# Another order of pieces, maxima and banks in the heads stage of a fused attention and experts kernel

## What is computed

```
xn = layernorm(x)
# branch 1: time mixing, then channel mixing
xc  = ln(ln(x2)); xcs = shift(xc)
kc  = square(relu(xcs @ Wck))            # 512 -> 2048, "up"
vc  = kc @ Wcv                           # 2048 -> 512, "down"
out1 = x2 + sigmoid(xc @ Wcr) * vc
# branch 2: causal attention in 4 x 16 heads of 32, then experts
p   = softmax(causal(q @ k.T * scale)); h = p @ v
x3  = xn + h @ Wo.T                      # "proj"
out2 = x3 + experts(rmsnorm(x3))
out = x + out1 + out2
```

## Time and profile before

| | |
|---|---|
| median of 3 executions | 1740.48 us (1737.22 to 1743.84) |
| the profiled execution, its own time | 1737.22 us |
| its span, first to last instruction | 1735.5 us |
| busy over the span: PE, DVE, ACT, POOL | 93%, 59%, 53%, 28% |
| mean granted TensorE clock | 0.983 |

### The profile page before, as it was taken

One profiled execution on the slowest core, in us unless ns is written; L12 is line 12 of the kernel. 1 busy time (PEld: TensorE's weight loads), 2 busy tenths in 40 slices (PEclk: granted clock), 3 DMA queues, 4 the chain that ended last, 5 costly groups with the idle time before them and its releaser, 6 DMA issues.

```text
span 1735.5 us, 26111 instructions
## 1 busy us (share of the span) xinstructions
PE 1621.6 (93%) x9014; PEld 1348.2 (78%) x9014; DVE 1021.1 (59%) x1980; ACT 917.4 (53%) x1649; POOL 480.0 (28%) x647
## 2 busy tenths in 40 slices
PE   3978899999989999999999899999999999999996
PEld 2756677877767777766768789898989898989895
DVE  7787742236665555655454655757565757575652
ACT  6465653334644655545643235656565656565652
POOL 4353320100111211211211312334342424252432
PEclk9999999999999999999999999999999999999998
DMA  6354576889796765974576665858585867676761
GB/s 239 101 172 150 214 216 188 240 253 311 229 291 190 212 193 121 297 222 124 155 233 213 213 190 193 281 201 269 199 275 200 271 221 252 235 239 229 246 230 25
DMA packets 119219, 370.12 MB, mean 213 GB/s; under 512 B 30175, under 2 KB 30175, under 8 KB 105378
## 3 DMA queue, kind: packets, MB, share of 16 engines
q1 hardware_dynamic: 98850, 329.36, 56.8%
q0 software_dynamic: 15696, 31.21, 9.7%
q10 hardware_dynamic: 4592, 8.52, 1.3%
HBM read 289.47 MB, written 85.72 MB: 216 GB/s over the span
## 4 chain that ended last, share of the span: by engine, by line
PE 64%; DVE 5%; ACT 3%; DMA 3%; issue 2%; SPq 1%; POOL 0%; DVEq 0%; POOLq 0%; ACTq 0%
PE bank L53 18%; PE bank L54 18%; PE bank L55 18%; PE bank L2283 3%; PE bank L2260 2%; PE bank L2248 2%; DVE ex_w_lo L2689 1%; DMA st_qk<-hd_max_rows 1%; DVE hd_a L2060 1%; PE bank L2792 1%; ACT hd_a_hi L1933 1%; DVE hd_masked L2120 1%; DMA st_qk<-scratch_qk 1%; PE bank L2352 1%; ACT hd_relu L1912 1%
## 5 line engine op out<-in xcount | busy, mean ns | idle before, releaser
L2689 DVE TENSOR_TENSOR ex_w_lo<-ex_stage,ex_w_hi 128x1024 fp32r<-128x1024 f32 x207 | 248.7, 1235 | 171.4 <-ACT ex_w_hi L2599 166.7
L2525 POOL TENSOR_TENSOR ex_a_lo<-ex_a,ex_a_hi 128x256 fp32r<-128x256 f32 x128 | 92.5, 746 | 292.9 <-ACT ex_a_hi L2621 292.7
L53 PE MATMUL bank<-ex_x_hi_a,ex_w_hi 128*128 128x256 f32 x512 | 145.0, 283 | 0.3 <-DVE ex_a L2727 0.3
L53 PE MATMUL bank<-ex_x_hi_b,ex_w_hi 128*128 128x256 f32 x512 | 144.6, 282 | 0.0
L55 PE MATMUL bank<-ex_x_hi_b,ex_w_lo 128*128 128x256 f32 x512 | 144.1, 282 | 0.0
L54 PE MATMUL bank<-ex_x_lo_a,ex_w_hi 128*128 128x256 f32 x512 | 144.1, 281 | 0.0
L55 PE MATMUL bank<-ex_x_hi_a,ex_w_lo 128*128 128x256 f32 x512 | 144.1, 281 | 0.0
L54 PE MATMUL bank<-ex_x_lo_b,ex_w_hi 128*128 128x256 f32 x512 | 144.1, 281 | 0.0
L2596 ACT ACTIVATE ex_w_hi<-ex_stage 128x1024 fp32r<-128x1024 f32 x134 | 133.8, 1049 | 0.6 <-DMA ex_stage<-in_w_moe 0.6
L2120 DVE CUSTOM_DVE_ANT_0 hd_masked<-bank,causal 128x512 bf16<-128x512 f32 (+3 forms) x256 | 113.8, 484 | 26.2 <-PE bank L2248 26.2
L53 PE MATMUL bank<-ex_w_hi,ex_a_hi 128*128 128x512 f32 x312 | 126.1, 404 | 0.3 <-DVE ex_w_lo L2689 0.3
(11 more groups left out here) (313 smaller groups left out, 4515.0 us busy)
## 6 DMA issues: line engine op xcount, KB each, us to landing
ex_stage<-in_w_moe SPq DMA_DIRECT2D x69, 1536.0 KB, 7.1
first_w<-in_w_moe SPq DMA_DIRECT2D x23, 1536.0 KB, 7.0
hd_up<-scratch_up_halves SPq DMA_DIRECT2D x48, 512.0 KB, 6.8
hd_down<-scratch_down_halves SPq DMA_DIRECT2D x48, 512.0 KB, 6.1
st_qk<-scratch_qk SPq DMA_DIRECT2D x64, 256.0 KB, 4.9
st_qk<-scratch_qk SPq DMA_DIRECT2D x128, 64.0 KB, 4.9
scratch_up_halves<-hd_up SPq DMA_DIRECT2D x16, 512.0 KB, 3.9
scratch_down_halves<-hd_down SPq DMA_DIRECT2D x16, 512.0 KB, 3.8
```

Source lines behind the costliest of these rows:

```text
L53: pe.matmul(out, lhsT=w_hi, rhs=x_hi, start=first, stop=False)
L2525: pool.tensor_tensor(a_lo[:, chunk.par, m, :], a[:, m, :], a_hi[:, chunk.par, m, :].bitcast(F32), ALU.subtract).then_inc(wide_lo_ready, 1)
L2689: return dve.tensor_tensor(dst, src, hi.bitcast(F32), ALU.subtract)
```

## The change

The order of work within a step and the banks of the pieces are changed; the work itself is the same.
- `pieces_before`: between step 5 and step 64 there are 85 pieces instead of 88, spread as 85 * n // 59 instead of 3 * n // 2, so steps with one and with two pieces no longer alternate strictly with odd and even s; after step 64 there are two in each step. The proj pieces of two sequences come a few pieces earlier in `order`.
- Banks: ups use bank 5 and sums bank 6 (two for each kind among the first pieces and from TAIL on). A piece waits for the last piece of its own kind instead of for piece k - 2.
- Order in a step, on all three engines: the first piece (also when it is the only one) is begun and finished ahead of scores, maxima and exps of part 2; the second piece stands behind them. `pair_output` comes after scores 2. `turn_maxima` and `max_row` come at the end of step 4t + 3 instead of in step 4t + 4.

```diff
     def pieces_before(s):
         early = 2 * min(s, LAG)
-        middle = 3 * min(max(s - LAG, 0), N - LAG) // 2
-        late = (3 * max(s - N, 0) + 1) // 2
+        middle = 85 * min(max(s - LAG, 0), N - LAG) // (N - LAG)
+        late = 2 * max(s - N, 0)
...
-        def piece_bank(k):
-            return psum[5 + k % 2]
+        TWO_UPS, TWO_SUMS = pieces_before(LAG + 1), pieces_before(LAG)
+
+        def up_bank(k):
+            return psum[4] if (k >= TAIL or k < TWO_UPS) and ups_before[k] % 2 else psum[5]
+
+        def sum_bank(k):
+            if k < TWO_SUMS:
+                return psum[2] if sums_before[k] % 2 else psum[6]
+            return psum[0] if k >= TAIL and sums_before[k] % 2 != sums_before[PIECES - 1] % 2 else psum[6]
... (scalar)
-                if s % SET == 0 and 0 < s <= N:
-                    max_row(s // SET - 1)
-                for k in ks[:-1]:
+                for k in ks[:1]:
                     begin(k)
+                    finish(k)
+                if 0 <= i < N:
+                    exps(i, 2)
                 if 1 <= i <= N and i % 2 == 0:
                     inverse_sums(i // 2 - 1)
-                if 0 <= i < N:
-                    exps(i, 2)
-                for k in ks[:-1]:
-                    finish(k)
                 (take_v, high_o)
-                for k in ks[-1:]:
+                for k in ks[1:]:
                     begin(k)
                     finish(k)
+                if s % SET == SET - 1 and s < N:
+                    max_row(s // SET)
... (vector)
-                for k in ks[:-1]:
+                for k in ks[:1]:
                     begin(k)
+                    finish(k)
                 if s < N:
                     maxima(s, 2)
-                for k in ks[:-1]:
-                    finish(k)
-                for k in ks[-1:]:
+                for k in ks[1:]:
                     begin(k)
                     finish(k)
... (tensor: an up piece; total() does the same with sum_taken)
-                if k >= 2:
-                    pe.wait_ge(*taken(k - 2))
+                n = ups_before[k] - (k > TAIL + TT or 0 < ups_before[k] and k < TWO_UPS)
+                if k >= TAIL and n == ups_before[TAIL]:
+                    pe.wait_ge(o_ready, N)
+                if n:
+                    pe.wait_ge(a_full, n)
... (tensor)
-                if s % SET == 0 and 0 < s <= N:
-                    turn_maxima(s // SET - 1, misc_free[0])
-                    misc_free[0] = max_rows_ready, s // SET
-                if 2 <= i <= N and i % 2 == 0:
-                    pair_output(i // 2 - 1)
-                for k in ks[:-1]:
+                for k in ks[:1]:
                     piece(k)
                 if s < N:
                     scores(s, 2)
+                if 2 <= i <= N and i % 2 == 0:
+                    pair_output(i // 2 - 1)
                 if 0 <= i < N:
                     turned(i, 2)
-                for k in ks[-1:]:
+                for k in ks[1:]:
                     piece(k)
+                if s % SET == SET - 1 and s < N:
+                    turn_maxima(s // SET, misc_free[0])
+                    misc_free[0] = max_rows_ready, s // SET + 1
```

More of the change, by code:

```diff
@@ L1911, in begin @@
                     act.wait_ge(up_done, n + 1)
-                    act.activation(relu[:, m, :], piece_bank(k)[:, :], ACT.Relu).then_inc(relu_ready, 1)
+                    act.activation(relu[:, m, :], up_bank(k)[:, :], ACT.Relu).then_inc(relu_ready, 1)
                 for w in fresh[k]:
@@ L2059, in begin @@
                     dve.wait_ge(relu_ready, n + 1)
-                    dve.scalar_tensor_tensor(a[:, m, :], piece_bank(k)[:, :], 0.0, relu[:, m, :],
+                    dve.scalar_tensor_tensor(a[:, m, :], up_bank(k)[:, :], 0.0, relu[:, m, :],
                                              ALU.max, ALU.mult).then_inc(a_full, 1)
@@ L2067, in begin @@
                         dve.wait_ge(added, 16 * adds_before[order.index(("down", b - 1, CHUNKS - 1, DEEP - 1)) + 1])
-                    dve.tensor_copy(acc[:, m, :], piece_bank(k)[:, :]).then_inc(sum_taken, 1)
+                    dve.tensor_copy(acc[:, m, :], sum_bank(k)[:, :]).then_inc(sum_taken, 1)
                 elif kind == "down":
@@ L2071, in begin @@
                     dve.wait_ge(sum_taken, before + 1)
-                    dve.tensor_tensor(acc[:, m, :], piece_bank(k)[:, :], acc[:, m, :], ALU.add).then_inc(sum_taken, 1)
+                    dve.tensor_tensor(acc[:, m, :], sum_bank(k)[:, :], acc[:, m, :], ALU.add).then_inc(sum_taken, 1)
                     if c == CHUNKS - 1:
@@ L2080, in begin @@
                         dve.wait_ge(xn_in, b * 16 + 16)
-                    dve.tensor_tensor(xp[:, m, :], piece_bank(k)[:, :], xp[:, m, :], ALU.add).then_inc(sum_taken, 1)
+                    dve.tensor_tensor(xp[:, m, :], sum_bank(k)[:, :], xp[:, m, :], ALU.add).then_inc(sum_taken, 1)
                 for w in fresh[k]:
@@ L2255, in turned @@
                     pe.wait_ge(max_in, 16 * (i // SET + 1))
+                if n == 0:
+                    pe.wait_ge(sum_taken, sums_before[TWO_SUMS])
                 if n >= 2:
@@ L2275, in pair_output @@
                     pe.wait_ge(consts_ready, CONSTS)
+                    pe.wait_ge(a_full, ups_before[TWO_UPS])
                 else:
@@ L2294, in up_piece @@
                     pe.wait_ge(x_in, b * 32 + 32)
-                if k >= 2:
-                    pe.wait_ge(*taken(k - 2))
+                n = ups_before[k] - (k > TAIL + TT or 0 < ups_before[k] and k < TWO_UPS)
[3 more added lines that the diff above has]
+                    pe.wait_ge(a_full, n)
                 for q in range(HC):
-                    last = mm3(pe, piece_bank(k)[:, :], up_hi[:, m, q, :], up_lo[:, m, q, :], x_hi[:, q, 1:S + 1],
+                    last = mm3(pe, up_bank(k)[:, :], up_hi[:, m, q, :], up_lo[:, m, q, :], x_hi[:, q, 1:S + 1],
                                x_lo[:, q, 1:S + 1], q == 0, q == HC - 1)
@@ L2302, in total @@
             def total(k, left_hi, left_lo, j, ready):
-                if k >= 2:
-                    pe.wait_ge(*taken(k - 2))
+                n = sums_before[k] - (k > TAIL or 0 < sums_before[k] and k < TWO_SUMS)
+                if k == TAIL:
+                    pe.wait_ge(max_step, 3 * N)
+                if n:
+                    pe.wait_ge(sum_taken, n)
                 cols = slice(j * P, (j + 1) * P)
@@ L2308, in total @@
                         ready(q)
-                    last = mm3(pe, piece_bank(k)[:, :], left_hi(q)[:, cols], left_lo(q)[:, cols], down_hi[:, q, :],
+                    last = mm3(pe, sum_bank(k)[:, :], left_hi(q)[:, cols], left_lo(q)[:, cols], down_hi[:, q, :],
                                down_lo[:, q, :], q == 0, q == DEEP - 1)
```

2 lines of the change are left out of this document (removed).

## The result

The changed kernel takes 1803.84 us, median of 4 executions (1801.71 to 1810.70), against 1739.19 for the kernel before beside it (4 executions, 1737.22 to 1743.84): a ratio of 1.0375, 95% interval 1.0338 to 1.0411. It is slower by 65 us. The forecast was 1783 with a range of 1754 to 1808.

What follows compares the result with a forecast made beforehand. TensorE was taken to bound the heads stage, the only one touched. New costs 44.2 + 11.8 + 6 + 8 + 8 = 78 us, less 32 removed, gave +46 on 1737.2: 1783 us, range 1754 to 1808.

Steps and rivals of the forecast that it cites:

- Part 1: Steps 5 to 63: TensorE's score part 1 waits for part 2 maxima, now behind the first piece on VectorE: 44.2 us.
- Part 2: One bank for ups, one for sums: a piece waits for the last of its own kind, 11.8 us together.
- Part 3: Late steps with two pieces each: pieces wait 0.5 to 1.0 at eight places, 6 us (bounds 0 and 8).
- Part 4: Row maxima turned earlier, their DMA issued most of a step sooner: removes 3.8 us of waits.
- Part 5: Moved neighbours ahead of part 2: `choose` in steps 28 and 62, 6 us; xT copies and logits waits, 2.
- Removed: Old TensorE waits in the heads stage undone by Parts 1, 4 and 5: 32 us (bounds 15 and 32).
- Clock: Five more drops of TensorE to half clock in the heads stage: 8 us (bounds 0 and 20).
- A: Heads stage slower as summed, only sizes of covers and chains open: 1765 to 1798 us, chance 0.66.
- B: Clock follows each long wait: some 12 drops more, 20 us on top, 1798 to 1820; sign ten; chance 0.12.
- C: Waits overlap, one late VectorE answer paying for several TensorE waits: +15, 1746 to 1765 us, chance 0.12.
- D: Faster: part 2 maximum not late on VectorE, Parts 1 and 5 cost nothing: -14, 1723 us, chance 0.05.
- E: No net change: old waits were TensorE's slack, new ones take their place: 1733 to 1745 us, chance 0.05.

Runs made afterwards that it cites:

- b1: The kernel before with only the new banks and bank waits of the pieces: 1770.30 us, ratio 1.0154.
- a2: The changed kernel with the banks and bank waits of the kernel before: 1792.55 us, ratio 1.0259.
- b3: The kernel before with only `turn_maxima` and `max_row` moved to the end of step 4t + 3: 1739.50 us, ratio 0.9987.
- e1: The changed kernel with the old banks and the old `pieces_before`, so only the order is new: 1742.67 us, ratio 0.9999.
- b2: The kernel before with only the new `pieces_before` layout: 1788.68 us, ratio 1.0257.
- a1: The changed kernel with VectorE doing the part 2 maxima ahead of the first piece, as before the change: 1778.22 us, ratio 1.0197.
- d2: d1 with the banks of the kernel before, still in the new layout: 1755.74 us, ratio 1.0068.
- d3: d2 with the old layout as well, so only the order is new, both queues mended: 1731.20 us, ratio 0.9934.
- g1: The changed kernel with ScalarE alone doing exps part 2 ahead of the first piece's finish in even steps: 1806.38 us, ratio 1.0381.
- d1: a1 plus ScalarE's edit of g1 (exps part 2 ahead of the first piece's finish in even steps): 1766.79 us, ratio 1.0151.
- f1: d3 with SP loading a slot ahead of following the step's second piece: 1728.51 us, ratio 0.9924.

## Why the prediction was right, and where it was off

The forecast was +46 us, and the measurement gave +65: inside the range, 21 us above the number. Term by term, read by starts as in the earlier trace rows (start to start, less the same pair unhindered):

- **Part 1, 44.2.** Right in place and size. Score 0 to score 1 shows 41.3 us too much, and the turning of maxima 2.5 in odd steps: 43.8. The forms agree too: step 5 2.80 and lone ups in even steps 2.83, 2.73 and 2.28 for 2.8, 4.54 for 4.8 where weight splits stand in between; behind a late up 3.04, 3.43, 2.56 for 3.3; most lone sums 0.8 to 0.9 for 0.8, and the two sums behind a late up 2.51 and 0.50 for 2.4. The profile's total for the score line, 39.0, is lower by what the modelled ends of matmuls cover.
- **Part 2, 11.8.** Right: 11.0, with 1.43 for two ups in an even step (1.33 forecast), 0.64 to 0.71 for two sums (0.7), and 0.63 for late up, then up (0.53), which shows in four of the seven places. On the old order, where these have less cover, the banks alone cost 27 (b1). The rule of the Trainium skill that independent groups should rotate through PSUM banks (Perfetto Trace Analysis, Matmuls) agrees with a2 and b1. The report that double buffering in PSUM gained nothing (TensorE: Matmul & The Clock Gate, HAM oscillation — how this bites in real kernels) does not carry over: here taking pieces of one kind by turns into two banks was worth 20 and 27 us.
- **Part 3, 6.** Right: 7.4 us by starts in nine places of the late steps, two of them behind a last up.
- **Part 4.** Right that the waits on `hd_max_rows` go; b3 shows no time for it that could be measured.
- **Part 5, 8.** Too high. Step 62, with `choose` in it, makes TensorE wait 4.60, of which 1.8 are `choose`; step 28 gives 0.34 in place of 3. Together some 2 us of the 6, and they are already in the 41.3. The other 2, for `xT` and logits, are right: 2.4 us are recorded, all at the turning of maxima.
- **Not in the sum.** The gate's DMA, 3.5 us at one place, below; a DMA of down weights, 0.9, and a low half of the attention output, 1.1.
- **Removed, 32.** Too high by 10, the largest part of the miss. The slot's DMA wait of 4.8 did go, but 3.5 us now stand at the gate's. By starts the old waits that vanished hold 28 us, and gaps of 0.1 to 0.2 us that were not there before hold some 6: 22 net, inside its bounds of 15 and 32.
- **Clock, 8.** Too low. The number of drops is right: nine stretches in place of four, and I took five more. But they are longer than the 3.4 us each that I took, 30.6 us more in all. Idle time inside them is counted above already; TensorE is busy for 24.4 us more of them (39.8 less 15.4), which at half speed is 12 us lost.

So 43.8 + 11.0 + 7.4 + 2.4 + 12 + 3.5 + 2.0 = 82 new, less 22, is 60, where the window grew by 59.4. These terms are read off one execution each and are good to a few us. Against the forecast of 46, the waits that I called removed give 10 us more, the clock 4, what was not in the sum 5.5, and part 5 gives 5.6 less: errors that partly cancel. The rest up to the measured 65 lies outside the window and in the spread of executions, for the profiled one took 1798.41 where the median is 1803.84.

A's mechanism holds, but the measured time is 6 us above A's range and falls into B's. B's sign was not seen: five more stretches (nine by their length) against its ten, and 12 us where it had some 28. So it was luck that the outer range, drawn to the middle of B, covers the result, with 4 us to spare. C falls (the waits did not overlap), and D and E with it. What was named ahead as the sign of each part was seen, but for the size of the window's growth (59 for 46): score waits over 35 us, ending at score 1, longest after lone ups in even steps; the bank waits; the stage longer and the experts not.

The gate's DMA, in the changed kernel (chain of work that ended last, from 521, then the busy times of that stretch, columns as in the earlier trace rows):

```profile
522.52 10.98 DMA hd_gate<-scratch_rc
...
533.52 0.04 DVE hd_acc L2080
...
534.13 0.42 DVE hd_masked L2123
...
534.62 0.60 PE bank L2274 x4
```

```profile
522.50:533.50 11.00, 8.84 (x46) 6.15 (x44) 4.31 (x12) 3.13 (x6) 3.22 (x5) 1.00 1.04 314
```

**One reading of mine was wrong, and the sum did not show it.** Part 1 was headed by the order on VectorE, as if putting the first piece ahead of the maxima were the fault. The experiments put the cost on the layout: with the old layout the new order costs nothing (e1), and the new layout costs 45 us in either order (b2, and a2 against e1). My arithmetic was right because it counted lone pieces in even steps, which the layout makes. Even steps have no pair output, 2.3 us of TensorE's work that waits for nobody in this chain; a lone piece there leaves 0.47 us of cover for an answer of 3.3. The order only decides whether score 1 or score 2 stands there. That mending VectorE's order (a1) gives back 31 us doesn't make it the cause: a1 is a third order, better than the new one in this layout. A better order does bear on it: with both queues mended the layout costs 23 us in place of 45.

What is not settled: how the 23 us between d2 and d3 divide. Recorded waits on row maxima are 12.0 us for 2.2, those on the two DMAs 10.1 for 5.2, those on low halves less (1.9 for 6.6), and the stage stands at half clock for 23.8 us in place of 10.2. Nor was the layout taken apart: that its cost comes from lone pieces in even steps, and not from where else it puts pieces, is read from where the waits stand and from no run of its own.

## What to carry to other kernels

When work that others must answer is spread over steps, look first at what stands beside it in each kind of step: a lone up piece cost 2.8 us of waiting for maxima where no pair output followed and at most 1.1 where one did. In queues that run in order, mend the longest wait first and then look again; an edit that is worth nothing alone (g1) can be worth something behind it (d1), and a DMA wait that is removed may only uncover the next DMA (f1). Compare each part both taken out of the new kernel and put alone into the old one: a mend that helps does not show that what it mends was the cause.

## What the runs showed of the hardware that was not expected

- The granted clock doesn't follow the length of single waits. By starts, waits of 2.8 us (ended at 428.52) and of 3.5 us (ended at 534.62) passed at 1.00, as did the recorded 2.42 of the earlier trace rows. A wait of 2.7 us that ended at 556.76 was followed by 0.50 at 557.0. At 625.2 the clock fell behind two short waits, 1.8 and 0.5 us, that ended at 624.29 and 625.07, and the wait of 3.4 us in that stretch came after the fall; at 707.2 it fell inside a wait of 4.5 us. The Trainium skill says that a TensorE that idles is brought to 1.2 GHz and must be kept busy to leave it (TensorE: Matmul & The Clock Gate, What's actually happening); the longer total at 0.50 with more idle time, 47.6 us for 17.0, agrees with that in direction. From the list of waits neither the places of the drops nor their length could be told ahead.
- A DMA can be very late: the one of the gate took 10.98 us in the changed kernel and 13.23 in f1, where the median of the sixteen such transfers in the changed kernel is 4.2 us. In both stretches the 16 DMA engines are fully busy (shares of 1.04 and 1.07). In the kernel before one of them took 11.9 us too.
